# Small tiles of a softplus chain in PSUM, waits written in another order, and a new order of steps

## The reference

```
h = group_norm(x, 8 groups)
q, k, v = h @ qkv_w.T                        # per image, 1024 tokens
a = softmax(q k.T / sqrt(128)) v @ proj_w.T + x
u = layer_norm(a)
z, xBC, dt = split(u @ in_w.T)               # 128, 128 + 2*64, 4 heads
dt = softplus(dt + dt_bias)
xs, B, C = silu(conv1d(xBC, 4 taps))
state_t = state_{t-1} * exp(dt_t * A) + dt_t * x_t * B_t ;  y_t = state_t . C_t
y = rms_norm((y + D * xs) * silu(z)) @ out_w.T
out = a + y * sigmoid(se2(relu(se1(mean(y)))))
```

## Time and profile before

| | us |
|---|---|
| runs (device time) | 291.04, 293.25, 295.36; median 293.25 |
| profiled execution: span, first to last instruction | 289.1 |
| busy in it: TensorE | 262.4 |
| busy: VectorE | 238.4 |
| busy: ScalarE | 210.1 |
| busy: GpSimd | 113.3 |

### The profile page before, as it was taken

How to read it: one execution, slowest core, us unless ns; L and a number is a source line. 1 busy time by engine, 2 the same in 40 slices (tenths; PEclk the granted TensorE clock), 3 DMA queues, 4 the chain that set the end, 5 groups by cost and what they waited for, 6 DMA issues and landing times. The chain is left out here.

```text
span 289.1 us, 6193 instructions
## 1 busy us (share of the span) xinstructions
PE 262.4 (91%) x1992; PEld 224.1 (78%) x1992; DVE 238.4 (82%) x517; ACT 210.1 (73%) x414; POOL 113.3 (39%) x114
## 2 busy tenths in 40 slices
PE   3999999999999999989899997899899996999691
PEld 2889978888887788778888696787898885576581
DVE  5795767447869899899999999989998998797933
ACT  2346678968999758859868974877587967888260
POOL 7000043152055201196454172333751166756171
PEclk9999999999999999999999999999999999999995
DMA  5920000040004400000265000330007100000013
GB/s 160 409 101 2 0 2 1 6 144 0 2 0 130 96 0 2 0 2 1 73 161 140 0 2 0 105 83 2 0 6 194 63 1 2 36 0 3 0 39 146
DMA packets 10987, 15.29 MB, mean 53 GB/s; under 512 B 1515, under 2 KB 5708, under 8 KB 10956
## 3 DMA queue, kind: packets, MB, share of 16 engines
q1 hardware_dynamic: 10412, 14.69, 16.3%
q10 hardware_dynamic: 544, 0.21, 0.3%
HBM read 12.70 MB, written 2.20 MB: 52 GB/s over the span
## 5 line engine op out<-in xcount | busy, mean ns | idle before, releaser
L1157 PEld LDWEIGHTS attn_out<-values,pT 128*128 128x128 f32 x512 | 62.1, 191 | 5.8 <-issue 4.5
L1157 PE MATMUL attn_out<-values,pT 128*128 128x129 f32 x512 | 65.5, 275 | 0.3 <-DVE res L985 0.3
L974 DVE TENSOR_REDUCE neg_max<-scores 128x1 f32<-128x1024 f32 x32 | 39.0, 1219 | 11.9 <-PE scores L1157 11.7
L649 ACT ACTIVATE probs<-scores,neg_max 128x512 f32<-128x512 f32 x64 | 41.6, 684 | 9.1 <-DVE neg_max L974 7.8
L655 ACT ACTIVATE pT<-turn 128x512 f32<-128x512 f32 x64 | 37.5, 594 | 11.3 <-PE turn L1230 11.0
L1230 PE MATMUL turn<-ident,probs 128*128 128x128 f32 x256 | 37.4, 274 | 1.7 <-ACT pT L655 1.7
L575 POOL TENSOR_TENSOR pre<-pre,th 128x512 f32<-128x512 f32 x16 | 22.0, 1373 | 42.6 <-ACT pre L681 39.6
L1230 PEld LDWEIGHTS turn<-ident,probs 128*128 128x128 f32 x256 | 29.9, 142 | 5.6 <-issue 3.5
L561 POOL TENSOR_TENSOR ln_rstd<-ln_var,neg_half 128x4 f32<-128x4 f32 x8 | 11.4, 1430 | 55.7 <-DVE ln_var L996 55.6
L1067 DVE TENSOR_TENSOR_SCAN L<-L,ident 128x512 f32<-128x512 f32 x24 | 28.9, 1219 | 0.7 <-DMA L<-decay_rows_d 0.7
L1157 PE MATMUL scores<-h_hi,q_hi 128*128 128x512 f32 x64 | 28.2, 441 | 0.6 <-DVE q_lo L970 0.6
(11 more groups left out here) (219 smaller groups left out, 606.4 us busy)
## 6 DMA issues: line engine op xcount, KB each, us to landing
L<-decay_rows_d SPq DMA_DIRECT2D x24, 256.0 KB, 3.9
res<-in_x_tok SPq DMA_DIRECT2D x4, 512.0 KB, 8.1
out<-res SPq DMA_DIRECT2D x8, 256.0 KB, 2.1
x_all<-in_x SPq DMA_DIRECT2D x3, 512.0 KB, 8.4
decay_in<-decay_rows_d SPq DMA_DIRECT2D x24, 64.0 KB, 3.6
x_all<-in_x SPq DMA_DIRECT2D x2, 256.0 KB, 3.1
winT<-in_in_wT SPq DMA_DIRECT2D x1, 194.0 KB, 6.9
wqkv<-in_qkv_w ACTq DMA_DIRECT2D x1, 192.0 KB, 4.0
```

Of the source, the lines that this page charges most:

```text
L649: act.activation(probs[:, i % 2, half_of(h)], scores[:, half_of(h)], ACT.Exp, bias=neg_max[:, i:i + 1]).then_inc(exp_done.sem, 1)
L974: V.tensor_reduce(neg_max[:, n:n + 1], scores[:, :], AX.X, ALU.max, negate=True).then_inc(max_ready.sem, 1)
L1157: return T.matmul(o, w, v, start=start, stop=stop)
```

## The change

Three things are done at once.

1. Tiles in PSUM. A function `beside` gives six slices of 16 columns at the start of the Dt bank. dte, the denominator and la_raw now lie there alone; dtx, s and dt are computed twice, once into SBUF and once into PSUM. Each VectorE instruction of the chain but the scan L864 takes at most one input from SBUF. The bank's reader is now the chain's ninth step.
2. In nearly every step with several waits, another one is written first.
3. `ORDER` is written anew, with other positions and other banks. It has the same 1281 steps.

```diff
-        "Dt": [(dtx_step, 1)],
+        "Dt": [(sp_step, SP_STEPS)],
...
+        def beside(b, n):
+
+            bank = mb[MAMBA_USES["Dt", n, b][0]]
+            return [bank[:, k * R:(k + 1) * R] for k in range(6)]
...
                 elif kind == "sp_exp":
                     wait(act, dta_ready, b, n + 1)
-                    act.activation(dte[:, n, :], dta[:, n, :], ACT.Exp, scale=-1.0)...
+                    dte = beside(b, n)[1]
+                    act.activation(dte, dta[:, n, :], ACT.Exp, scale=-1.0)...
...
             def softplus(b, n, k):
                 by_head = lambda a: a.rearrange("p (c h) -> p c h", h=HEADS)
                 s = sp_s[:, n, :]
+                dtx_too, dte, den, s_too, dt_too, la_raw = beside(b, n)
                 if k == 0:
-                    return V.tensor_scalar(sp_den[:, n, :], dte[:, n, :], 2.0, None, ALU.add)
+                    return V.tensor_scalar(den, dte, 2.0, None, ALU.add)
                 if k == 1:
-                    return V.reciprocal(s, sp_den[:, n, :])
+                    return V.reciprocal(sp_r[:, n, :], den)
                 if k == 2:
-                    return V.tensor_tensor(s, s, dte[:, n, :], ALU.mult)
+                    V.tensor_tensor(s_too, dte, sp_r[:, n, :], ALU.mult)
+                    return V.tensor_tensor(s, dte, sp_r[:, n, :], ALU.mult)
                 if k == 3:
-                    twice = s.unsqueeze(2).broadcast_to([P, R, TERMS - 1])
-                    return V.tensor_tensor(sp_s2[:, n, :, 1:TERMS], twice, twice, ALU.mult)
+                    one, other = (a.unsqueeze(2).broadcast_to([P, R, TERMS - 1]) for a in (s_too, s))
+                    return V.tensor_tensor(sp_s2[:, n, :, 1:TERMS], one, other, ALU.mult)
...
                 if k == 5:
-                    return V.scalar_tensor_tensor(sp_log[:, n, :], sp_sum[:, n, :, TERMS - 1], 2.0, s, ALU.mult, ALU.mult)
+                    return V.scalar_tensor_tensor(sp_log[:, n, :], s_too, 2.0, sp_sum[:, n, :, TERMS - 1], ALU.mult, ALU.mult)
                 if k == 6:
-                    return V.scalar_tensor_tensor(dt[:, n, :], dtx[:, n, :], 0.0, sp_log[:, n, :], ALU.max, ALU.add)
+                    V.scalar_tensor_tensor(dt_too, dtx_too, 0.0, sp_log[:, n, :], ALU.max, ALU.add)
+                    return V.scalar_tensor_tensor(dt[:, n, :], dtx_too, 0.0, sp_log[:, n, :], ALU.max, ALU.add)
                 if k == 7:
-                    return V.tensor_tensor(by_head(la_raw[:, n, :]), by_head(dt[:, n, :]),
+                    return V.tensor_tensor(by_head(la_raw), by_head(dt_too),
                                            a_neg[:, :].unsqueeze(1).broadcast_to([P, QUAD, HEADS]), ALU.mult)
-                return V.tensor_scalar(la[:, n, :], la_raw[:, n, :], DA_LOG_MIN * A_SCALE, None, ALU.max)
+                return V.tensor_scalar(la[:, n, :], la_raw, DA_LOG_MIN * A_SCALE, None, ALU.max)
...
                 elif kind == "dt_x":
                     bank = take(dve, b, "Dt", n)
+                    dtx_too = beside(b, n)[0]
+                    for to in (dtx[:, n, :], dtx_too):
+                        ins = V.tensor_tensor(to..., ALU.add)
+                    ins.then_inc(dtx_step.sem, 1)
                     wait(dve, dtx_step, b, n + 1)
-                    V.scalar_tensor_tensor(dta[:, n, :], dtx[:, n, :], -1.0, dtx[:, n, :], ALU.mult, ALU.max
+                    V.scalar_tensor_tensor(dta[:, n, :], dtx_too, -1.0, dtx[:, n, :], ALU.mult, ALU.max
...
                 elif kind == "u":
+                    bank = take(act, b, "UT", n)
                     for use in ("InX", "InBC", "InZ", "Dt"):
                         wait(act, filled[use], b - 1, n + 1)
-                    bank = take(act, b, "UT", n)
...
                 if kind == "Q":
+                    wait(pe, exp_done, b - 1, 15 + n)
+                    wait_h_lo(pe, b, n + 1)
+                    wait(pe, h_hi_ready, b, n + 1)
                     pe.wait_ge(kq_ready.sem, 1)
-                    wait(pe, h_hi_ready, b, n + 1)
-                    wait_h_lo(pe, b, n + 1)
-                    wait(pe, exp_done, b - 1, 15 + n)
```

About thirty steps have their waits turned round in the way of the last two. Of the order, the beginning, and the queues of SP (as the list gives them) in batch c and after:

```diff
-gn_stats0 warm3 gn_mm10 kq_mm gn_dev0 gn_mm20 vp_mm gn_ve0 kq_ev gn_pow0 gn_aff0 h0a h_hi0a h1a h_hi1a h_lo0a h_lo1a
-warm5 Q0a vp_ev Q1a q_hi0a V0a@0 ...
+kq_mm gn_stats0 gn_mm10 warm3 gn_dev0 gn_mm20 warm5 kq_ev gn_ve0 gn_pow0 vp_mm gn_aff0 h_hi0a h0a h1a h_lo0a h_hi1a
+h_lo1a win_s vp_ev Q0a Q1a q_hi0a ...
-SP: wr0c bc0c bc1c bc2c bc3c dd0c wr1c bc4c store0a dd1c bc5c bc6c bc7c store1a store0b
+SP: wr0c dd0c bc0c bc1c bc2c bc3c wr1c bc4c bc5c bc6c store0a dd1c bc7c store1a store0b
```

More of the change, by code:

```diff
@@ L68 @@
[L68 to L77, removed]
@@ new lines @@
+stc0c inv3d res3d th_x1c Yo0c@2 zt1c stats3d PV8d ln_ve0d pl0b bc4c pT9d bc5c ln_pow0d zv1c PV9d T10d@0 bc6c gate0c
+Pl1b@1 u_tok0d UT0d@0 max6d exp12d xs1c l4c th_bc1c T11d@1 S14d u0d yo0c pl1b inv4d InBC0d@0 Dt0d@1 store0a silu1c
+exp13d dd1c bc7c raw_bc0d pT10d c1c l5c InX0d@2 yo_dx0c XsT1c@0 S15d res4d PV10d T12d@0 dt_x0d l6c term0d pT11d PV11d
+l7c xdt1c max7d raw_x0d SeA0b@0 to_end1c conv_bc0d pT12d term1d inv5d sp_exp0d hdn0b sp0d G1c@2 sp1d SeB0b@0 res5d
+exp14d tha0b m4c T13d@0 sp2d T14d@1 conv_bc1d BT1c@0 m5c PV12d xend1c stats4d bt1c gated0b m6c U1c@0 pT13d fin1a m7c
@@ L640, in step @@
                 elif kind == "v":
+                    bank = take(act, b, "V", n)
                     wait(act, pv_done, b - 1, 16)
-                    bank = take(act, b, "V", n)
                     act.activation(values[:, QUAD * n:QUAD * (n + 1), 0:P],
@@ L652, in step @@
                     i, h = divmod(n, 2)
+                    bank = take(act, b, "T", n)
                     wait(act, pv_done, b, n - 3)
-                    bank = take(act, b, "T", n)
                     act.activation(pT[:, i % 2, QUAD * h:QUAD * (h + 1), :],
@@ L670, in step @@
                     k, name, use, bias = (0, "x", "InX", BX) if kind == "raw_x" else (1, "bc", "InBC", BBC)
+                    bank = take(act, b, use, n)
                     wait(act, tap[name], b - 1, 2 * PAD)
-                    bank = take(act, b, use, n)
                     act.activation(raw[:, k, PAD + n * HALF:PAD + (n + 1) * HALF], bank[:, :], ACT.Identity,
@@ L799, in step @@
                 elif kind == "hdn":
+                    bank = take(act, b, "SeA", 0)
+                    wait(act, filled["SeB"], b - 1, 1)
                     act.wait_ge(zeros_done.sem, 5)
-                    wait(act, filled["SeB"], b - 1, 1)
-                    bank = take(act, b, "SeA", 0)
                     act.activation(hdn[0:SE, :], bank[0:SE, 0:1], ACT.Relu, bias=vec[0:SE, SE1B:SE1B + 1],
@@ L1055, in step @@
                     rows = slice(R * n, R * (n + 1))
+                    bank = take(dve, b, "XsT", n)
                     wait(dve, sp_step, b, SP_STEPS * n + SP_DT)
@@ L1058, in step @@
                     wait(dve, xend_ready, b - 1, n + 1)
-                    bank = take(dve, b, "XsT", n)
                     V.tensor_tensor(xdt[:, rows, :], bank[:, :].rearrange("p (a b) -> p a b", b=HEADDIM),
@@ L1093, in step @@
                     part = slice(P, HALF) if n == 0 else half
+                    bank = take(dve, b, "Yo", n)
                     if by_dma(b):
@@ L1099, in step @@
                     wait(dve, xs_ready, b, n + 1)
-                    bank = take(dve, b, "Yo", n)
                     V.tensor_tensor(yo[:, part], bank[:, P if n == 0 else 0:HALF], decay_in[:, part], ALU.mult
@@ L1117, in step @@
                 elif kind == "y":
+                    bank = take(dve, b, "Y", n)
                     wait(dve, yo_dx_ready, b, n + 1)
@@ L1120, in step @@
                     wait(dve, o_sum_ready, b - 1, n + 1)
-                    bank = take(dve, b, "Y", n)
                     V.tensor_tensor(y[:, half], bank[:, :], yo[:, half], ALU.add).then_inc(y_ready.sem, 1)
@@ L1362, in step @@
                 elif kind == "Pl":
-                    bank, done = fill(pe, b, "Pl", n)
                     if b < BATCH - 1:
@@ L1370, in step @@
                         tiles = [o_tok[:, QUAD * n + k, :] for k in range(QUAD)]
+                    bank, done = fill(pe, b, "Pl", n)
                     for k, t in enumerate(tiles):
```

210 lines of the change are left out of this document (106 added, 104 removed).

## The result

The changed kernel takes 276.16 us in the median of four runs (275.92 to 276.65), the kernel before 293.35 in the runs beside them (291.04 to 295.36). The ratio is 0.943 with a 95% interval of 0.938 to 0.949: faster by 17.2 us in the medians, 16.5 by the ratio. Some runs of a kernel are slower at a lower granted clock (the kernel before: 295.5 us at 0.97 beside 290.7 at 0.99); the medians and ranges here hold them, the ratios leave them out.

The account below looks back on a forecast made before the run. It took TensorE to bound the kernel before 100 us and VectorE's queue after. 5.8 + 0.9 + 0.4 + 0.8 - 0.5 = 7.4 us off 293.25 gave 285.85, rounded 286; range 280 to 292 for 8 in 10.

Parts of the forecast that it names:

- Operands to PSUM: Softplus chain: six small VectorE lines stop stalling beside GpSimd, 11.9 us removed over five chains from 100 to 248 us.
- I take three quarters: From 100 to 248 us: three quarters of the 7.8 us taken off VectorE becomes time, 5.8 us; bounds 2.0 to 9.3.
- Added instructions: Softplus chain: second dtx, s and dt on VectorE at 0.17 us each, 0.51 a chain, 2.6 us for five.
- The penalty of PSUM sources: Eleven chain instructions reading PSUM: the skill's fixed cost would be 0.7 us a chain, 3.5 for five; not counted.
- Stalls that move on: VectorE's next two-SBUF-input instructions meet the rest of the GpSimd one: 0 to 4.0 us lost, 1.5 taken.
- The bank held longer: Dt bank, free only after the chain's ninth step: cost taken as 0, the order being laid out for it.
- the second rival: Held Dt bank: 46 fills have two banks, not three; at 0.25 us each, 11.5 us, giving 297; chance 0.09.
- Waits: Engine queues: writing the latest wait first takes semaphore pieces off the path; 0 to 4.3 us, 0.8 taken.
- The first: Rival: saved time becomes VectorE idle time, only pieces on the path count, 2.4 us, giving 291; chance 0.20.
- The third: Rival: every VectorE microsecond passes on and the queue pieces go too, 13.7 us, giving 279.5; chance 0.17.
- The fourth: Rival: small instructions still block on the write side, 4.1 us added and nothing saved, giving 296; chance 0.04.
- Prologue: Start: three warming matmuls move between the group-norm products; second product and scores' start about 0.5 us later.

Follow-up runs that it names:

- e13: The kernel before with three more copies of dtx a chain, 24 VectorE instructions in all; 295.33 us, ratio 1.011 to the kernel before.
- e3_order: The kernel before with only the new ORDER, positions and banks; tiles in SBUF, waits as before; 284.11 us, ratio 0.973 to the kernel before.
- e12: The changed kernel with three more copies of dtx a chain, 24 in all; 277.08 us, 1.5 us above the changed kernel (-0.4 to 3.5).
- e1: The changed kernel with the softplus tiles back in SBUF, new waits and order kept; 282.61 us, ratio 0.969 to the kernel before.
- e5: The kernel before, re-banked so Dt banks are held to the ninth step, 12 fills and o1b moved, tiles in SBUF; 301.40 us, ratio 1.034.
- e4: The list of e5 with the tiles in PSUM, waits as before; 298.63 us, ratio 1.020 to the kernel before.
- e9: e3_order with each fill given the bank whose last reader comes earliest in the list, 96 differ; 284.76 us, ratio 0.974 to the kernel before.
- e10: The kernel before with the new order up to batch c's first scores, old order behind; 297.14 us, ratio 1.018 to the kernel before.
- e11: The kernel before with the old order up to batch d's first scores, new order behind; 289.17 us, ratio 0.989 to the kernel before.
- e15_moves_old: The positions of e5, but each fill takes the bank whose last reader comes earliest, Dt banks not held; 293.35 us, ratio 1.005 to the kernel before.
- e6_waits: The kernel before with the changed kernel's waits alone; 293.07 us, ratio 1.007 to the kernel before.
- e8_banks_old: The kernel before, positions kept, each fill given the bank whose last reader comes earliest, 108 entries differ; 294.76 us, ratio 1.012.

## Why the prediction failed, step by step

**What bounds the kernel: held in the main.** VectorE's queue from 100 us on, and stalls inside its instructions: 24 instructions more on it cost 3.2 us (e13). Ahead of 100 us the order gained too, and there it was not VectorE's busy time.

**Operands to PSUM: mechanism right, sum right by two errors.** The lines are at 0.17 to 0.18 us beside GpSimd. The two terms for the tiles, 5.8 and 0.9, with 0.4 for batch a's chains, made 7.1; 6.4 to 7.4 was measured on the new order. That is luck. But the 11.9 us to remove were read from the old order. In e3_order the order had already taken 9.0 of them, and what was left paid more than forecast elsewhere: L859, which I had not among the six lines of the stretch, was 550 ns in the mean there. The share that becomes time, "I take three quarters", is no constant: 0.3 to 0.4 on the held old list (2.8 us of span, 3.9 in the runs, of 10.0), 1.0 on the new.

**Added instructions: too dear.** 0.17 each, 2.6 us for five chains, should have been some 0.08, 1.2 us (e12).

**The penalty of PSUM sources: not seen.** The Trainium skill (VectorE: DVE Perf Modes, "The TRN2 errata") would have had 0.7 us a chain, by the estimate of the prediction. L860 takes 170 ns in the mean from PSUM, where L855 takes 166 from SBUF undisturbed in e3_order; L877 183, where the median of L871 in e3_order is 176. By these rows the difference is below 20 ns an instruction. The measurement decides, and the net was rightly made without it.

**Stalls that move on: partly.** 1.5 us were priced. From e1 to the changed kernel the scan got 1.4 us longer in its eight instructions and the large groups next to it as much shorter (`x_all` 0.9, `pre` 0.6): nothing net. From e5 to e4 the scan got 1.5 us longer, `pre` 0.9 and the L scan 1.2.

**The bank held longer, at 0: right for this list, but the stated reason doesn't carry it.** On the new list nothing can be seen (e9 to e3, 0.3 us, -2.4 to 3.1). The prediction's reason, and its case against the second rival, was that the next user of each held bank stands behind the ninth step. That is just as true of e5's list, and there the banks cost 8.4 us, 0.16 a fill, right at the price from which the rival would decide. What the lists differ in is where the other fills stand (46 inside the chains against 53); which of that spares the new list isn't shown.

**Waits: 0.8 forecast, 1.4 to 2.3 measured.** Inside the bounds of 0 to 4.3. That upper bound was not a sound one: the chain of the earlier trace rows, from whose 0% it was made, covers 34% of the span. How waits are issued was read rightly, though it is 43 kinds of step that have their waits turned round, not about thirty: the wait for `kq_ready` in step Q is written first in the kernel before (L1200) and has no record of its own, and last in the changed kernel (L1212), where it has eight, seven of them 0.05 us long.

**The rivals.** The first (saved time becomes VectorE's idle time) isn't seen on the new list, where the span less VectorE's busy time went from 50.7 to 46.9 us, and is what e4 shows on the old one. The second is above. The third, everything passes on, gave 279.5 and came nearest, by luck too, for it had nothing for the order. The fourth falls with the rows at 0.17 (and its own sum, 293.25 and 4.1, is 297.3 and not 296).

**Prologue.** The scores of batch a start at 12.26 us instead of 12.07: 0.2 late, not 0.5.

**The step that failed: "For the rest of the reordering and the banks I count 0, with 3 us to either side; no row prices that."** It is worth 7.8 us with the prologue's 0.5 in it (6.6 to 9.0; 8.6 in the medians), more than twice the 3 us that the sentence allows. The sentence was wrong about the rows as well. The earlier trace rows show that a collision depends on what stands at the same time in two queues. A list that moves GpSimd's and VectorE's steps against one another changes just that, and it had up to 11.9 us to work on. And TensorE's 2.13 us without work ahead of 100 us were there to be taken: the prediction read that stretch as one that the attention fills. A fair bound, as an estimate from these two numbers, would have been 0 to 14. The sum by parts: forecast were 7.1 for the tiles, 0.8 for the waits and -0.5 for the order, together 7.4; measured are 7.4, 1.4 and 7.8, together 16.6, and 8.3 of the 9.2 between the two sums are the order's.

**What stays open.** That the positions do it is shown (e3, e9). That they lower VectorE's busy time by fewer collisions is shown by the groups. That they are not the whole of it is likely: 20 of the 44 matmuls by which e3_order leads at 200 us are there by 100 us, where VectorE is as busy as before and TensorE's idle time of 2.13 us is nearly gone. How much each of the two is worth isn't shown: both come with the same list, and the halves (e10, e11) don't separate. Which of the moves carry it was not found.

## What to carry to other kernels

When a change contains a new order, price the order from the traces as a part of its own: take every microsecond of stall inside instructions, and every gap of the next engine, as what it could remove, before calling it 0. Two parts that remove the same stall don't add, and how much of a saved microsecond reaches the end depends on the list, from a third to all of it here. A tile parked in a bank isn't free because the bank's next user stands behind its last reader: that held on both lists, and the banks cost 8.4 us on the old one and nothing that could be seen on the new. Time the new list without the tiles first, as e3 and e5 do here.

## What was not expected of the hardware

- Small VectorE instructions that are independent start 0.06 to 0.09 us apart although each record is 0.17 us long (e12). The price in the queue is half of the mean that the groups show.
- The scan with two SBUF inputs can be held by GpSimd too. In the changed kernel its longest one (start, duration, instruction):

```profile
77.31 1.27 POOL L578 TENSOR_TENSOR pre<-pre,x_all 128x512 f32<-128x512 f32 x1
...
77.41 1.45 DVE L870 TENSOR_TENSOR_SCAN sp_sum<-sp_s,sp_coef 128x128 f32<-128x128 f32 x1
```

  It starts 0.10 us after GpSimd's `pre`, which ends at 78.58, and ends 0.28 us behind that. The one at 194.03 ends 0.29 us behind the end of xend at 194.36. The Trainium skill (SBUF — State Buffer, "Who interferes with whom") says that the order of issue decides who blocks, not the shape of the instruction, and that the other blocks fully, and these two rows agree. Not every meeting goes so. In the kernel before a scan starts at 205.55 us with 0.25 us left of y_rstd (4 elements a partition), and isn't held; there the measurement decides.
- Which of the two is held can turn on a few hundredths of a microsecond. The same scan and the same GpSimd instruction, in the kernel before and in e15_moves_old:

```profile
232.10 1.51 POOL L575 TENSOR_TENSOR pre<-pre,x_all 128x512 f32<-128x512 f32 x1
232.13 0.41 DVE L864 TENSOR_TENSOR_SCAN sp_sum<-sp_s,sp_coef 128x128 f32<-128x128 f32 x1
```

```profile
232.27 1.27 POOL L575 TENSOR_TENSOR pre<-pre,x_all 128x512 f32<-128x512 f32 x1
232.30 1.53 DVE L864 TENSOR_TENSOR_SCAN sp_sum<-sp_s,sp_coef 128x128 f32<-128x128 f32 x1
```

  Both times the scan starts 0.03 us behind the GpSimd instruction. In the first GpSimd is held and the scan runs its 0.41, in the second the scan is held. e6_waits and e8_banks_old have it as in the second. So a single meeting puts 1.1 us into VectorE's busy time or leaves it out, and a difference of 1 or 2 us between two such totals says little until the meetings are compared.
- A 16-element tile read from PSUM or from SBUF makes a difference below 20 ns (170 against 166).
